# A 27-feature interaction tower on one core: third raw table buffer, one-product bias, layer 2 of tile three reordered

## The reference, cut to what matters

```python
e = jnp.stack([tbl_f[ids[:, f]] for f in range(26)], axis=1)      # 512 x 26 x 128, f32
combined = concatenate([dense[:, None, :], e], axis=1)              # 512 x 27 x 128
inter = einsum('bfd,bgd->bfg', combined, combined)[:, iu, ju]       # 351 pairs per sample
h = concatenate([dense, inter, dense], axis=1)                      # 512 x 607
h = maximum(h @ W_top1 + b_top1, 0)                                 # 512 x 512
h = maximum(h @ W_top2 + b_top2, 0)                                 # 512 x 256
y = h @ W_top3                                                      # 512 x 1
```

## Time and profile before

| | |
|---|---|
| median of three runs | 112.67 us |
| the profiled execution's own time | 112.72 us |
| its span, first to last instruction | 111.0 us |
| granted TensorE clock | 1.00 of full speed throughout |
| PE busy | 103.1 us (93%) |
| DVE busy | 79.7 us |
| ACT busy | 74.0 us |
| POOL busy | 71.9 us |

### The profile page before, as it was taken

The page is one execution under the profiler, slowest core; times in us unless marked ns, Lnnn a source line. Parts: engine busy times, 40 slices in busy tenths (PEclk is TensorE's granted clock), DMA queues, the critical chain, the costliest instruction groups (busy, mean ns, idle before and its releaser), DMA issues.

```text
span 111.0 us, 1932 instructions
## 1 busy us (share of the span) xinstructions
PE 103.1 (93%) x670; PEld 90.3 (81%) x670; DVE 79.7 (72%) x184; ACT 74.0 (67%) x131; POOL 71.9 (65%) x73
## 2 busy tenths in 40 slices
PE   3999999699999999989999989999999999999971
PEld 3965788577888888667999979999999998988760
DVE  5389999959999998972177996988348750596421
ACT  3347988999999999698578754759342563744030
POOL 6977778778877777777777777777777772000000
DMA  1899876892598279994211122112221111000000
GB/s 42 247 285 348 260 248 180 321 301 66 159 289 310 64 294 269 368 350 125 56 47 47 47 62 59 50 47 53 56 62 47 47 47 47 6 0 3 0 0 1
DMA packets 7195, 14.74 MB, mean 133 GB/s; under 512 B 1937, under 2 KB 2578, under 8 KB 7186
## 3 DMA queue, kind: packets, MB, share of 16 engines
q1 hardware_dynamic: 4850, 10.36, 27.9%
q0 software_dynamic: 2048, 4.20, 14.0%
q10 hardware_dynamic: 288, 0.07, 0.3%
HBM read 14.62 MB, written 0.00 MB: 132 GB/s over the span
## 4 chain that ended last, share of the span: by engine, by line
PE 50%; ACT 20%; DMA 13%; DVE 10%; issue 3%; SPq 1%; ACTq 0%; DVEq 0%
PE gram L450 25%; DMA table<-in_tbl 13%; ACT eT L703 7%; ACT table_hi L703 6%; DVE onehot L909 5%; PE late L552 5%; PE late L501 4%; DVE table_lo L903 3%; ACT distance L719 3%; PE look L426 3%; ACT onehot L723 2%; PE gram L529 1%; PE late L415 1%; PE look L529 1%; PE late L416 1%
## 5 line engine op out<-in xcount | busy, mean ns | idle before, releaser
L369 POOL DMA_INDIRECT e_rows<-in_gathered,idx x64 | 68.4, 1068 | 19.4 <-issue 19.4
L415 PE MATMUL late<-onehot,table_hi 128*128 128x512 f32 x84 | 34.3, 409 | 2.2 <-ACT eT L703 1.4
L416 PE MATMUL late<-onehot,table_lo 128*128 128x512 f32 x84 | 33.2, 395 | 0.0
L450 PE MATMUL gram<-eT 128*123 128x108 f32 x256 | 29.6, 271 | 0.6 <-ACT dots L703 0.3
L909 DVE TENSOR_SCALAR onehot<-ids,row_of_partition 128x512 fp32r<-128x512 int32 x69 | 29.8, 480 | 0.3 <-DMA ids<-in_ids_bcast 0.3
L450 PEld LDWEIGHTS gram<-eT 128*123 128x123 f32 x256 | 28.6, 187 | 1.0 <-ACT eT L703 0.5
L415 PEld LDWEIGHTS late<-onehot,table_hi 128*128 128x128 f32 x84 | 16.0, 190 | 8.0 <-ACT eT L703 2.3
L680 DVE COPY dots<-gram 32x216 f32<-32x216 f32 (+3 forms) x34 | 12.6, 371 | 11.2 <-PE gram L450 10.7
L703 ACT ACTIVATE dots<-gram 32x216 f32<-32x216 f32 (+1 forms) x34 | 11.2, 330 | 11.9 <-PE gram L450 11.7
L416 PEld LDWEIGHTS late<-onehot,table_lo 128*128 128x128 f32 x84 | 16.1, 191 | 3.0
L903 DVE TENSOR_TENSOR table_lo<-table,table_hi 128x384 fp32r<-128x384 f32 (+2 forms) x29 | 15.5, 536 | 2.7 <-ACT table_hi L703 2.7
(11 more groups left out here) (103 smaller groups left out, 112.9 us busy)
## 6 DMA issues: line engine op xcount, KB each, us to landing
table<-in_tbl SPq DMA_DIRECT2D x7, 512.0 KB, 3.6
ids<-in_ids_bcast SPq DMA_DIRECT2D x10, 256.0 KB, 4.0
w_raw<-in_w SPq DMA_DIRECT2D x7, 256.0 KB
table<-in_tbl SPq DMA_DIRECT2D x2, 640.0 KB, 3.8
e_rows<-in_gathered,idx POOLq DMA_INDIRECT x64, 2.8
table<-in_tbl SPq DMA_DIRECT2D x2, 256.0 KB, 4.1
x_rows<-in_dense SPq DMA_DIRECT2D x1, 256.0 KB, 4.7
w_sb<-in_w SPq DMA_DIRECT2D x1, 128.0 KB
```

The costliest lines, as they stand in the source:

```text
L369: pool.indirect_dma_start(out=e_rows[:, c % GROUPS_AHEAD, k, :], out_offset=None, in_=gathered[:, :], in_offset=bass.IndirectOffsetOnAxis( ...
L415: pe.matmul(bank, table_hi[0:KP, i % 2, c, :], hot, start=c == 0, stop=False)
L416: last = pe.matmul(bank, table_lo[0:KP, i % 2, c, :], hot, start=False, stop=c == CHUNKS[i] - 1)
L450: last = pe.matmul(gram[0:ROWS_OUT, n % 2, q, 0:QUADS * NG_COL], eT_flat[:, b * SLOTS:b * SLOTS + ROWS_OUT], eT[:, b:b + QUADS, 0:NG_COL], ...
```

## The change

Four things are altered.

1. `table` gets three buffers in place of two (`RAW_RING = 3`). Load i waits for the lo pieces of table i - 3. `table_hi` and `table_lo` keep two.
2. The bias of layer 2: `b2` is loaded to 33 partitions, its rounded value goes to partitions 0 to 32 of `b2_rows`, whose partition 32 is then replaced by the rest; all other partitions are zero. `bias_rows` has ones in partitions 0 and 32 and zeros elsewhere. One product over 128 partitions takes the place of two over one. Four `memset`s on DVE make the constants, ahead of DVE's wait for the weights.
3. PE's order at the end: two of the four steps of layer 2 of tile 2 (k = 2 and 3) move behind layer 1 of tile 3. `layer3(2)` on DVE moves behind `h1_rows_rest`. The turned h1 of tile 3 goes to `gram` banks and has semaphores of its own.
4. In `layer2_rows_3` the products with `h1_hi` come first and wait for it alone; those with `h1_lo` follow.

```diff
-                if i >= 2:
-                    sp.wait_ge(lo_ready, pieces_split(LO_PIECES, i - 2))
-                sp.dma_start(table[0:KP, i % 2, 0:c, :],
-                             padded[i].rearrange("(p c) d -> p c d", c=c)).then_inc(table_in[i % 2], 16)
+                if i >= RAW_RING:
+                    sp.wait_ge(lo_ready, pieces_split(LO_PIECES, i - RAW_RING))
+                sp.dma_start(table[0:KP, i % RAW_RING, 0:c, :],
+                             padded[i].rearrange("(p c) d -> p c d", c=c)).then_inc(table_in[i % RAW_RING], 16)
...
-            sp.dma_start(b2_sb[:, :], b2).then_inc(w_in, 16)
+            sp.dma_start(b2_sb[:, :], b2.to_broadcast([LO_ROW + 1, H2])).then_inc(w_in, 16)
...
+        def h1_bank(n):
+            if n == 2:
+                return look[:, LOOK["h1", n] % 2, :]
+            q = CHUNK_Q // 2 if n == 3 else 0
+            return gram[:, 4 - n, q:q + N1, :].rearrange("b q n -> b (q n)")
...
-                pe.matmul(layer2_bank(t), one_row[0:1, :], b2_hi[0:1, :], start=True, stop=False)
-                pe.matmul(layer2_bank(t), one_row[0:1, :], b2_lo[0:1, :], start=False, stop=False)
+                pe.matmul(layer2_bank(t), bias_rows[:, :], b2_rows[:, :], start=True, stop=False)
...
             def layer2_rows_3():
-                wait_look_done(pe, ("h1", 3))
-                for k in (2, 3):
-                    layer2_step(3, k, False)
-                wait_look_done(pe, ("h1", 4))
-                for k in (0, 1):
-                    last = layer2_step(3, k, k == 1)
+                t = TILES - 1
+                rows = slice(t % 2 * P, (t % 2 + 1) * P)
+                for n, ks in ((3, (2, 3)), (4, (0, 1))):
+                    pe.wait_ge(h1_hi_ready, n + 1)
+                    for k in ks:
+                        pe.matmul(layer2_bank(t), h1_hi[:, k, rows], w2_hi[:, k, :], start=False, stop=False)
+                        pe.matmul(layer2_bank(t), h1_hi[:, k, rows], w2_lo[:, k, :], start=False, stop=False)
+                    pe.wait_ge(h1_last_lo, n - 2)
+                    for k in ks:
+                        last = pe.matmul(layer2_bank(t), h1_lo[:, k, rows], w2_hi[:, k, :], start=False,
+                                         stop=n == 4 and k == ks[-1])
                 last.then_inc(last_full, 1)
...
-            layer2_rows_2((0, 1))
+            layer2_rows_2((0,))
             turn_last_pairs(0)
-            layer2_rows_2((2,))
+            layer2_rows_2((1,))
             turn_last_pairs(1)
             turn_last_pairs(2)
-            layer2_rows_2((3,))
             layer2_bias(3)
             layer1_rows_3()
+            layer2_rows_2((2,))
             turn_h1(3, (2, 3))
             turn_h1(4, (0, 1))
+            layer2_rows_2((3,))
             layer2_rows_3()
...
+            dve.memset(b2_rows[:, :].bitcast(F32), 0.0).then_inc(bias_zero, 1)
+            dve.memset(bias_rows[:, :].bitcast(F32), 0.0).then_inc(bias_zero, 1)
+            dve.wait_ge(bias_zero, 2)
+            dve.memset(bias_rows[0:1, :].bitcast(F32), 1.0).then_inc(bias_zero, 1)
+            dve.memset(bias_rows[LO_ROW:LO_ROW + 1, :].bitcast(F32), 1.0).then_inc(bias_zero, 1)
             dve.wait_ge(w_in, 16 * W_LOADS)
...
-            copy(one_row[:, :], one_col[0:1, :])
-            copy(b2_hi[:, :], b2_sb[:, :]).then_inc(w_hi, 1)
+            act.wait_ge(bias_zero, 4)
+            copy(b2_rows[0:LO_ROW + 1, :], b2_sb[:, :]).then_inc(w_hi, 1)
...
             turn_lo(3)
-            layer3(2)
             relu_rows_3()
             h1_rows_rest(3, slice(2, N1))
             h1_rows_rest(4, slice(0, 2))
+            layer3(2)
             layer3(3)
```

More of the change, by code:

```diff
@@ L137 @@
 LOOK_ORDER += [("group", 11), ("group", 12), ("layer2", 0), ("group", 13), ("turn", 2)]
-LOOK_ORDER += [("group", 14), ("group", 15), ("h1", 2), ("group", 16), ("turn", 3), ("layer2", 2), ("h1", 3), ("h1", 4)]
+LOOK_ORDER += [("group", 14), ("group", 15), ("h1", 2), ("group", 16), ("turn", 3)]
 LOOK = {what: n for n, what in enumerate(LOOK_ORDER)}
@@ L182, in build @@
         e_rows = sb("e_rows", [P, GROUPS_AHEAD, GROUP, P])
-        table = sb("table", [P, 2, MAXC, P])
+        table = sb("table", [P, RAW_RING, MAXC, P])
         table_hi = sb("table_hi", [P, 2, MAXC, P], F32R)
@@ L224, in build @@
         table0_in = [sem(f"table0_in{k}") for k in range(2)]
-        table_in = [sem(f"table_in{k}") for k in range(2)]
+        table_in = [sem(f"table_in{k}") for k in range(RAW_RING)]
         x_in = sem("x_in")
@@ L263, in build @@
         pT_lo_ready = sem("pT_lo_ready")
+        h1_last_full = sem("h1_last_full")
+        h1_last_lo = sem("h1_last_lo")
+        third_full = sem("third_full")
         y_ready = sem("y_ready")
@@ L374, in build @@
         eT_flat = eT[:, :, :].rearrange("d b s -> d (b s)")
+        def h1_bank(n):
[3 more added lines that the diff above has]
+            return gram[:, 4 - n, q:q + N1, :].rearrange("b q n -> b (q n)")
         def late_layer2(t):
+            if t == 2:
+                return look[:, LOOK["group", NCK] % 2, 0:H2]
             q = 0 if t == TILES - 1 else CHUNK_Q // 2
@@ L518, in layer2_bias @@
             def layer2_bias(t):
-                if t in (0, 2):
+                if t == 0:
                     look_bank(("layer2", t))
+                elif t == 2:
+                    wait_look_done(pe, ("group", NCK))
                 else:
@@ L591, in turn_h1 @@
             def turn_h1(n, ks):
-                bank = look_bank(("h1", n))
+                if n == 2:
+                    look_bank(("h1", n))
+                bank = h1_bank(n)
                 wait_late_done(pe, ("rows", n))
@@ L595, in turn_h1 @@
                     last = pe.transpose(bank[:, k * P:(k + 1) * P], h1_rows[:, k * P:(k + 1) * P], ident[:, :])
-                last.then_inc(look_full, 1)
+                last.then_inc(look_full if n == 2 else h1_last_full, 1)
             def layer2_rows_2(ks):
@@ L711, in split_hi @@
                     else:
-                        act.wait_ge(table_in[i % 2], 16 * (i // 2 + i % 2))
-                    copy(table_hi[0:KP, i % 2, a:c, :], table[0:KP, i % 2, a:c, :]).then_inc(hi_ready, 1)
+                        act.wait_ge(table_in[i % RAW_RING], 16 * len([j for j in range(1, i + 1) if j % RAW_RING == i % RAW_RING]))
+                    copy(table_hi[0:KP, i % 2, a:c, :], table[0:KP, i % RAW_RING, a:c, :]).then_inc(hi_ready, 1)
             def one_hot(i, c):
@@ L842, in h1_rows_split @@
                     act.wait_ge(last_full, 1)
-                wait_look_full(act, ("h1", n))
+                if n == 2:
+                    wait_look_full(act, ("h1", n))
+                else:
+                    act.wait_ge(h1_last_full, n - 2)
                 copy(h1_hi[:, ks, t % 2 * P:(t % 2 + 1) * P],
-                     look[:, LOOK["h1", n] % 2, :].rearrange("n (k b) -> n k b", k=N1)[:, ks, :]).then_inc(h1_hi_ready, 1)
+                     h1_bank(n).rearrange("n (k b) -> n k b", k=N1)[:, ks, :]).then_inc(h1_hi_ready, 1)
             dots_chunk(0)
@@ L1020, in h1_rows_rest @@
                 dve.tensor_tensor(h1_lo[:, ks, cols],
-                                  look[:, LOOK["h1", n] % 2, :].rearrange("n (k b) -> n k b", k=N1)[:, ks, :],
-                                  h1_hi[:, ks, cols].bitcast(F32), ALU.subtract).then_inc(look_dve, 1)
+                                  h1_bank(n).rearrange("n (k b) -> n k b", k=N1)[:, ks, :],
+                                  h1_hi[:, ks, cols].bitcast(F32), ALU.subtract
+                                  ).then_inc(look_dve if n == 2 else h1_last_lo, 1)
             def h1_rest(h):
@@ L1038, in layer3 @@
                 else:
-                    dve.wait_ge(last_full, 1 + t // 2)
+                    if t == 2:
+                        dve.wait_ge(third_full, 1)
+                    else:
+                        dve.wait_ge(last_full, 1 + t // 2)
                     bank = late_layer2(t)
@@ L1042, in layer3 @@
                                                 op0=ALU.max, op1=ALU.mult, accum_out=y[:, t:t + 1])
-                done.then_inc(look_dve if t in (0, 2) else y_ready, 1)
+                done.then_inc(y_ready if t else look_dve, 1)
             dots_chunk(0)
```

26 lines of the change are left out of this document (14 added, 12 removed).

## The result

The changed kernel takes 109.06 us (median of four runs, 108.88 to 109.52) against 112.74 us (112.50 to 113.73) before: a ratio of 0.966, with a 95% interval of 0.960 to 0.973. So 3.0 to 3.7 us were gained where 3.5 were forecast. The six later runs of the changed kernel span 1.6 us, and the eleven of the kernel before beside them 0.6; but in two other sets the kernel before spans 1.5 and 1.1 us, so no difference in spread is shown.

A forecast was written before the change was run, and what follows sets the result against it. PE was taken as the bound, with pauses from late table loads, a relay at the end and gathers at their own pace. 112.72 - 1.1 (ahead of the tail) - 1.92 (tail) - 0.46 (hi first) = 109.24 us, range 108.4 to 110.4.

The forecast's parts named there:

- Part 1, tables: Table stage: a third raw buffer removes ACT's waits for tables 3 and 9; Gram products start 1.5 us earlier.
- Part 2, the bias: Layer 2: bias and successor take 0.24 us in place of 0.74, saving 0.50 for each of four tiles.
- tile 0's 0.5 us: Ahead of group 14: tile 0's bias saving, making PE 2.0 us early in place of 1.5, limited only by gathers.
- The gathers' limit: Transposes of group 14: PE can be only 1.1 us earlier; the other 0.9 returns as a wait for gathers.
- Part 3, the tail: Tail: three biases (1.50) and six moved products (0.71), less a 0.29 stall at the band: 1.92 us earlier.
- Part 4, hi first: Layer 2 of tile 3: products needing ACT alone fill 0.47 us until `h1_lo` is there; 0.46 us saved.
- Sum: Whole kernel: 1.1 ahead of the tail, 1.92 and 0.46 taken from 112.72 us, giving 109.24.
- (c): Layer 2's bias: pauses come from opening a bank, 0.12 saved in place of 0.50; 110.4 us, chance 0.08.
- (b): Ahead of the tail: gathers come earlier with a shorter table stage, PE keeps 1.6 of 2.0; 108.7 us, chance 0.12.
- (a): Front gives nothing: tables land no sooner or gathers are delayed by about 1.1 us; 110.0 us, chance 0.13.
- (d): Table stage: early loads slow the gather stream, so the kernel gets slower; 113.7 us at a 4.5 us shift, chance 0.04.

The follow-up runs named there:

- after_again: The changed kernel with no edit, run again later: 109.61 us, ratio 0.976 to the kernel before.
- bias_pair: The changed kernel with layer 2's bias as two products over one partition again: 110.28 us, ratio 0.976 to the kernel before.
- both_waits: The changed kernel with the transposes of tile 2's band moved behind Gram chunk 13 and gather 41 left out: 109.06 us, ratio 0.967 to before.
- steps_back: The changed kernel with PE's order of the end, and `layer3` of tile 2 on DVE, as before the change: 110.05 us.
- lo_waited: The changed kernel with all twelve products of layer 2 of tile 3 waiting for `h1_lo` again, order still hi then lo: 109.66 us.
- ring3_only: The kernel before with the third raw table buffer alone: 112.36 us over twelve runs, ratio 0.995 to before.
- bias_33: The changed kernel with the bias product over 33 partitions in place of 128: 109.79 us in one run.
- bias_twice: The changed kernel with its full bias product issued twice into the same bank: 109.75 us in one run.
- small_loads: The changed kernel with the loads of tables 4 to 9 cut to one or two of their 8 or 10 chunks: 109.83 us in one run.
- pairs_behind: The changed kernel with the three transposes of tile 2's band moved on PE behind Gram chunk 13: 109.28 us.

## Why the prediction was right

**Part 1, tables.** ACT's idle time ahead of tables 3 and 9 is gone. I took 1.5 us as ready at the Gram products; the profiled execution has 1.66. Some of it is the execution's own: kernels whose code up to there is the changed kernel's started their Gram products between 50.90 and 52.02.

**Part 2, the bias.** 0.12 us between starts, as forecast, and the two control kernels show the mechanism, one run each. In R to L it is worth 1.02 us alone. The step that failed is tile 0's 0.5 us: I added it to what PE brings to group 14 (2.0 us) and let only the gathers take it. It arrived in no stretch. G to R is 44.07 us with it (after_again, with no gather waited for) and 44.12 without (bias_pair), since the transposes of tile 2's band wait for `layer3` of tile 0, the last piece of a DVE chain that starts with Gram chunk 11 and doesn't get shorter with PE's work. I had looked for the next limit among the gathers alone. No run let both limits go (both_waits was to, but met gather 60), so that the 0.5 us would arrive without them is not shown.

**The gathers' limit.** I put PE's room at group 14 at 1.1 us. The table confirms the number: before, R stood 5.85 us behind gather 64, and the least is 4.7. The changed kernel's R came 1.56 us earlier and not 1.1 because its stream was 0.42 us earlier (90.77 against 91.19), within the half microsecond that I had left to POOL. PE had some 2.1 us to bring (1.66 and 0.5), so 0.6 was lost, where I expected 0.9 at gather 60: 0.4 went at DVE's chain and 0.15 at gather 60.

**Part 3, the tail.** Forecast 1.92 us, measured 1.73. Each edit alone is as I had it: from before to steps_back, which has the new bias and the old order, R to L falls from 7.26 to 5.81, 1.45 us against my 1.50; from before to bias_pair, with the new order and the old bias, from 7.26 to 6.55, 0.71 against 0.71. Together they give 1.73, so 0.43 is lost where I had 0.29: PE now meets the band. By the timeline the product ahead of the first transpose starts at 98.16, the transpose at 98.60, 0.32 more than the usual 0.12 (my own starts, 99.74 and 100.07, gave 0.33, and I took 0.29); the rest goes at the second pair and behind it, where the bias product takes 0.18, as this chain of the changed kernel has it:

```profile
99.26 0.29 PE gram L486 x2
99.55 0.18 PE gram L540
99.73 2.15 PE late L567 x18
```

**Part 4, hi first.** Forecast 0.46, measured 0.53 (lo_waited). The moved steps are free, as L to E of steps_back says. The gap of 0.43 us that I gave them is 0.48 by the numbers beside it (105.50 less 105.02), which changes nothing.

**Sum.** 1.1 + 1.92 + 0.46 = 3.48 against 1.56 + 1.73 + 0.52 = 3.81. Without the luck of 0.42 us in the gathers it would have been 3.4. Of the rivals, (c) fell to bias_pair. (b) is what the profiled execution did ahead of the tail (1.56 us kept, 1.6 in the rival), but by its own early stream and not by a stage that is shorter in every execution. (a) is what some executions of ring3_only look like. (d) did not come: over the eleven profiled executions with three buffers and all gathers, gather 64 is issued at 91.1 on average, as in the two with two buffers (91.19, 91.01), though single ones lie 1.3 us to either side. Something of (d) can be seen all the same: from gather 32 to gather 64 the stream takes 40.7 to 40.8 us in those eleven and 40.2 to 40.3 in the two. The half microsecond lies in two gathers near 55 to 58 us, as here in the changed kernel; why, no run shows.

```profile
55.02 1.22 POOL L374 DMA_INDIRECT e_rows<-in_gathered,idx  x1 [0.30 <-issue]
56.55 1.33 POOL L374 DMA_INDIRECT e_rows<-in_gathered,idx  x1 [0.30 <-issue]
```

## What to carry to other kernels

When an engine is made faster, hold its new room against every stream and every chain that keeps its own pace: issue + landing against use gave the gathers' limit to 0.1 us, though no wait named it before, and a bank freed at the end of a long chain on DVE held PE as well. When executions differ by more than an edit is worth, compare stretches between marks in the traces, not medians.

## What the runs showed of the hardware that I had not expected

A product over 33 partitions between products over 128 costs PE about 0.38 us beyond its own 0.12 (bias_33, starts at 96.39, 96.60, 96.91 and 97.13), and the pair over one partition cost the same beyond its own 0.24 (0.74 with its successor, before); a second full product adds 0.12 (bias_twice).

The gather stream is not the same twice. The same 64 gathers ended with an issue at 89.85 in one execution and at 91.71 or 92.39 in others, with no edit on POOL. In the table stage the instruction takes 0.94 to 1.79 us, and which gather gets which length changes from execution to execution: the changed kernel has one of 1.78 us, small_loads, with gather 64 at 91.68, has two of 1.79.

```profile
17.95 1.78 POOL L374 DMA_INDIRECT e_rows<-in_gathered,idx  x1 [0.30 <-issue]
```

Before, the stream had 1.1 us of room at group 14, so that such a change could stay hidden; in the changed kernel it can move the end, as R of pairs_behind and small_loads shows. That it makes the runs lie further apart is not shown.
